# Feed-forward activations turned by transposing DMAs out of 16-bit halves instead of on TensorE

## The reference

```python
x = embeddings                                   # (8, 1024, 512) f32
x = layernorm(x + attention(x, w_qkv))
# feed-forward, I = 1408; fq = blockwise FP4 quantise and dequantise, 16 values per scale
gate = einsum('bsk,nk->bsn', fq(x), fq(w_gate))
up   = einsum('bsk,nk->bsn', fq(x), fq(w_up))
h    = silu(gate) * up
x = layernorm(x + einsum('bsk,nk->bsn', fq(h), fq(w_down)))
```

## Time and profile before

| what | value |
|---|---|
| median of 3 executions | 3875.96 us (3875.09 to 3875.98) |
| the profiled execution | 3875.39 us, its span 3873.6 us |
| PE busy | 3689.6 us, 95% of the span |
| DVE busy | 3168.6 us, 82% |
| POOL busy | 2203.6 us, 57% |
| ACT busy | 1711.3 us, 44% |
| granted TensorE clock, mean of the span | 0.989 of full speed |

### The profile page before, as it was taken

The page is one execution under the profiler, slowest core; times in us unless marked ns, Lnnn a source line. Parts: engine busy times, 40 slices in busy tenths (PEclk is TensorE's granted clock), DMA queues, the critical chain, the costliest instruction groups (busy, mean ns, idle before and its releaser), DMA issues.

```text
span 3873.6 us, 60731 instructions
## 1 busy us (share of the span) xinstructions
PE 3689.6 (95%) x22282; PEld 1713.6 (44%) x22469; DVE 3168.6 (82%) x5203; ACT 1711.3 (44%) x3084; POOL 2203.6 (57%) x1395
## 2 busy tenths in 40 slices
PE   3599999999999999999999999999999999999999
PEld 2244454344544445443554445434454345544354
DVE  9877888778877788778877788777887778877887
ACT  2166523664246632566226652366424663256622
POOL 1289623984249832698228962388424983269822
PEclk9699999999999999999999999999999999999999
DMA  5211101011011110111101110101101111010110
GB/s 171 79 39 31 58 20 39 18 41 50 23 34 30 38 47 20 41 27 31 52 25 37 32 58 20 39 18 42 50 23 34 30 38 47 20 41 26 34 49 23
DMA packets 106551, 152.38 MB, mean 39 GB/s; under 512 B 28176, under 2 KB 55568, under 8 KB 106128
## 3 DMA queue, kind: packets, MB, share of 16 engines
q1 hardware_dynamic: 106256, 148.49, 12.4%
HBM read 76.28 MB, written 19.66 MB: 25 GB/s over the span
## 4 chain that ended last, share of the span: by engine, by line
PE 76%; DVE 13%; issue 2%; ACT 2%; POOL 2%; DMA 1%; SPq 0%; DVEq 0%; ACTq 0%; POOLq 0%
PE SC L1646 15%; PE CT L1586 10%; PE R L699 9%; PE SC L1571 8%; PE R L679 7%; DVE mx L605 6%; PE CT L1668 6%; PE R L1668 6%; PE R L1646 5%; PE R L689 4%; PE R L711 2%; PE R L1606 2%; PE R L721 1%; POOL wd L1168 1%; DVE split L599 1%
## 5 line engine op out<-in xcount | busy, mean ns | idle before, releaser
L605 DVE TENSOR_REDUCE mx<-R 128x1 f32<-128x512 f32 x2080 | 1315.1, 683 | 344.6 <-PE R L699 339.9
L1285 ACT ACTIVATE arena<-SC 128x512 f32<-128x512 f32 x1364 | 756.6, 602 | 351.1 <-PE SC L1571 321.2
L1646 PE MATMUL SC<-wgu,split 128*128 128x512 f16 (+1 forms) x3456 | 714.5, 361 | 0.0
L1168 POOL TENSOR_TENSOR wd<-wd,arena 128x1024 f32<-128x1024 f32 x224 | 535.1, 2414 | 77.2 <-DVE wd L1407 77.2
L1194 POOL TENSOR_TENSOR arena<-arena,sc_h 128x704 f32<-128x704 bf16 (+1 forms) x144 | 178.4, 1253 | 605.7 <-DVE arena L528 605.7
L1646 PEld LDWEIGHTS SC<-wgu,split 128*128 128x128 f16 x3456 | 338.0, 98 | 331.6
L1327 ACT ACTIVATE arena<-SC,gain 128x512 f32<-128x512 f32 (+1 forms) x192 | 125.2, 652 | 810.1 <-PE R L1646 411.7
L1285 ACT ACTIVATE wd<-SC 128x512 f32<-128x512 f32 x684 | 387.5, 602 | 200.4 <-PE SC L1571 188.3
L679 PE MATMUL R<-xT,wqkv 128*128 128x512 bf16 x1509 | 398.2, 382 | 27.7 <-DVE xT L592 14.8
L699 PE MATMUL R<-ks_even,qs_even 96*128 96x512 bf16 x1056 | 394.9, 389 | 18.1 <-DVE mx L605 8.3
L699 PE MATMUL R<-arena 96*128 96x512 bf16 x1024 | 374.0, 382 | 14.6 <-DVE xT L592 6.5
(11 more groups left out here) (139 smaller groups left out, 5397.0 us busy)
## 6 DMA issues: line engine op xcount, KB each, us to landing
x<-n_L_attn_embeddings_dram SPq DMA_DIRECT2D x136, 256.0 KB, 2.7
wd<-wd_kept SPq DMA_DIRECT2D x32, 512.0 KB, 5.6
out_dram<-x SPq DMA_DIRECT2D x64, 256.0 KB, 2.0
ks_even<-split SPq DMA_DIRECT2D x204, 64.0 KB, 2.0
qs_even<-split SPq DMA_DIRECT2D x408, 32.0 KB, 1.9
arena<-split SPq DMA_DIRECT2D x192, 64.0 KB, 2.0
arena<-split SPq DMA_DIRECT2D x384, 32.0 KB, 1.9
wd<-wd_kept SPq DMA_DIRECT2D x16, 384.0 KB, 7.2
```

The lines of the kernel that those rows point to most:

```text
L605: nc.vector.reduce_max(mx[:, j:j + 1], ring_of(ring, job)[:, :], AX_X).then_inc(max_done, 1)
L1168: nc.gpsimd.tensor_tensor(acc[u % 2][i], acc[u % 2][i], probs_of(s)[:, hs, :], ALU.add).then_inc(pool_sum, 1)
L1285: nc.scalar.activation(probs_of(s)[:, hd, :], SC[e % SLOTS][:, :], ACT.Exp, scale=SCALE).then_inc(exp_done, 1)
L1646: last = nc.tensor.matmul(GU[kk % 2][which][:, 0:w], xhT[i % 2][:, part_x * KH + k, :], wgu[:, part_w * KH + k, which * I + first:which * ...
```

## The change

The turns leave PE. q_x and q_h are split into halves while they still lie untransposed in SBUF: ACT copies the high half (`x_high`, `h_high`), POOL subtracts to get the low half (`low_x`, `low_h`, which were DVE's), and SP issues one transposing DMA for the two halves of x together (128 x 1024 of 16 bits) and one for each piece of h. The pieces of h are now 768 and 640 columns, so the DMAs are 128 x 1536 and 128 x 1280; in tiles 0 and 7 they are 1024, 1024 and 768 wide. `xs` lies over xn, and `hs` over a spare stretch of the arena. The orders of all five engines change with it. ACT runs `x_high(i+1)` after silu(i, 2) and both `h_high(i-1)` between silu(i, 0) and silu(i, 1). POOL runs scale_x(i+1), inverse_deviation of the output norm of tile i-2, low_x(i+1), inverse_deviation for x, scale_h of both pieces, low_h of both. SP runs the h turns of tile i-1, the x turn of tile i+1, then the load and the store. At the head, `x_high(0)` stands ahead of the context copy on ACT, and the DMA for x(0) stands behind `stack_maxima` on SP. Of the last tile's projections, the second follows down's second chunk and the rest the third. DVE's add of y is earlier in the last tile.

```diff
-H_PIECES = (slice(0, I // 2), slice(I // 2, I))
+H_PIECES = (slice(0, 6 * P), slice(6 * P, I))
...
+        xs = xn.bitcast(F16)
+        hs = spare.bitcast(BF16)
...
+                    def turn_x(i):
+                        i += TILES * b
+                        sp.wait_ge(xs_lo, i + 1)
+                        if i >= 2:
+                            sp.wait_ge(gu_done, len(CHUNKS) * (i - 1))
+                        sp.dma_start_transpose(xhT[i % 2], xs).then_inc(xhT_loaded, 16)
+
+                    def turn_h(i):
+                        i += TILES * b
+                        for n, (first, k) in enumerate(tile_pieces(i)):
+                            sp.wait_ge(hs_lo, pieces(i)[n][0] + 1)
+                            if i >= 2 and n == 0:
+                                sp.wait_ge(y_done, i - 1)
+                            sp.dma_start_transpose(hT[i % 2][:, 2 * first:2 * (first + k), :],
+                                                   hs[:, 2 * first * P:2 * (first + k) * P]).then_inc(hT_loaded[n], 16)
+
+                    turn_x(0)
                     keep_x(0)
-                    for c in range(len(CHUNKS)):
+                    load_down(b, 0)
+                    turn_x(1)
+                    for c in range(1, len(CHUNKS)):
                         load_down(b, c)
-                    for i in range(TILES):
+                    keep_x(1)
+                    for i in range(1, TILES):
+                        turn_h(i - 1)
                         if i + 1 < TILES:
+                            turn_x(i + 1)
                             keep_x(i + 1)
...
+                def low_x(i):
+                    pool.wait_ge(xs_hi, i + 1)
+                    nc.gpsimd.tensor_tensor(xs[:, H:2 * H], q_x, xs[:, 0:H], ALU.subtract).then_inc(xs_lo, 1)
...
+                def low_h(i, n):
+                    k, cols = pieces(i)[n]
+                    high, low = halves_of(cols)
+                    pool.wait_ge(hs_hi, k + 1)
+                    nc.gpsimd.tensor_tensor(hs[:, low], q_h[:, cols], hs[:, high], ALU.subtract).then_inc(hs_lo, 1)
...
+                def x_high(i):
+                    act.wait_ge(qx_done, i + 1)
+                    nc.scalar.activation(xs[:, 0:H], q_x, ACT.Copy).then_inc(xs_hi, 1)
+
+                def h_high(i, n):
+                    k, cols = pieces(i)[n]
+                    act.wait_ge(qh_done, k + 1)
+                    if i >= 1 and n == 0:
+                        h_turned(act, i - 1)
+                    nc.scalar.activation(hs[:, halves_of(cols)[0]], q_h[:, cols], ACT.Copy).then_inc(hs_hi, 1)
...
                     if c == 0 and which == 0:
-                        pe.wait_ge(xhT_done, i + 1)
+                        pe.wait_ge(xhT_loaded, 16 * (i + 1))
...
+                        if k == at:
+                            pe.wait_ge(hT_loaded[n], turned_until(i, n))
```

More of the change, by code:

```diff
@@ L384, in in_chunks, with tile_pieces, turned_until, halves_of @@
             return i % TILES in (0, TILES - 1)
+        def tile_pieces(i):
+            return [(c.start // P, (c.stop - c.start) // P) for _, c in pieces(i)]
+        def turned_until(i, n):
+            b, i = divmod(i, TILES)
+            return 16 * ((TILES if n < len(H_PIECES) else 2) * b + 1 + (i if n < len(H_PIECES) else i // (TILES - 1)))
+        def halves_of(cols):
+            w = cols.stop - cols.start
+            return slice(2 * cols.start, 2 * cols.start + w), slice(2 * cols.start + w, 2 * cols.stop)
+        def h_turned(eng, i):
+            for n in range(len(pieces(i))):
+                eng.wait_ge(hT_loaded[n], turned_until(i, n))
         def rounds_before(i):
@@ L447, in post_ln_block @@
         qh_done = sem("qh_done")
-        hT_hi = sem("hT_hi")
-        hT_done = sem("hT_done")
+        hs_hi = sem("hs_hi")
+        hs_lo = sem("hs_lo")
+        hT_loaded = [sem(f"hT_loaded{n}") for n in range(len(CHUNKS))]
         y_done = sem("y_done")
@@ L1219, in tiles @@
                             inverse_deviation("out", at + i - 2)
+                        if 1 <= i < TILES - 1:
+                            low_x(at + i + 1)
                         if 1 <= i < TILES - 2:
                             inverse_deviation("x", at + i + 2)
-                        for n in range(len(pieces(at + i))):
-                            scale_h(at + i, n)
+                        if in_chunks(i):
+                            for n in range(len(CHUNKS)):
+                                scale_h(at + i, n)
+                                low_h(at + i, n)
+                        else:
+                            for n in range(len(H_PIECES)):
+                                scale_h(at + i, n)
+                            for n in range(len(H_PIECES)):
+                                low_h(at + i, n)
                     for i in range(TILES - 3, TILES):
@@ L1350, in tiles @@
-                        if i > at:
-                            h_out(i - 1, 2)
-                        if i + 2 < at + TILES:
-                            first_norm(i + 2)
-                    i = at + TILES - 1
-                    h_out(i, 0)
-                    second_norm(i - 2)
+                        if i + 2 <= last:
+                            first_norm(i + 2)
+                    silu(last, 0)
+                    for n in range(len(pieces(last - 1))):
+                        h_high(last - 1, n)
@@ L1453, in units @@
                             first_moments(TILES * b + 1)
[L1455 to L1462, removed]
-                    nc.vector.tensor_tensor(hT[i % 2][:, first + tiles:first + 2 * tiles, :],
-                                            ring_tiles(ring, ("hT", i, c), tiles),
-                                            hT[i % 2][:, first:first + tiles, :], ALU.subtract).then_inc(hT_done, 1)
                 def quantise_h(i, cols):
```

192 lines of the change are left out of this document (61 added, 131 removed).

## The result

The changed kernel takes 3805.12 us (3804.19 to 3807.41 in 4 runs) against 3875.55 us of the kernel before beside it (3875.09 to 3875.98, 4 runs). The ratio is 0.982 (0.9808 to 0.9832): 70.4 us or 1.8% faster, where I had forecast 30 us. The profiled execution took 3805.33 us, its span 3803.6 us.

A forecast was written before the change was run, and what follows sets the result against it. PE was taken as the bound, DVE a close second. Per batch 2.6 - 0.44 + 6 x (22.5 - 23.15) - 2.4 = -4.1 us, -33 over 8 batches; forecast 3846 us, range 3775 to 4070.

The forecast's parts named there:

- PE alone sets the pace: Rival, middle tiles: DVE and POOL pass more freely, period 21.4 us from PE's matmuls, 3790 us; chance 0.13.
- The period: Middle tiles, gate_up to gate_up: 22.5 us instead of 23.15, or 22.85 with the dearer POOL price.
- DVE's own sum: DVE per middle tile: 18.2 us bare work, 3.3 of waits and some 0.5 more of stalls, 22.0 us.
- DVE and POOL shut each other out: Middle tiles: small scalar instructions and SBUF passes wait for POOL, and POOL for them; 3.3 us of waits, formerly 0.75.
- POOL's price: POOL's added subtractions per tile: 1.65 and 1.4 us for the pieces of h, 1.2 for x.
- The landing time L: Transposing DMA of 256 KB inside SBUF, from issue to landing: taken as 3.0 us.
- the transposing DMA becomes the wait: Rival, gate_up(i+1) behind turn_x(i+1): slower if L exceeds about 4.3 us; 3968 at L = 6, 4044 at 7.2; chance 0.36.
- its extreme: Transposing DMA paid block by block: 30 blocks of a tile take 39 us, kernel about 1000 us slower.
- 18.9 + L: Middle-tile period in the DMA rival, with stalls, as the chain to turn_x plus landing time; break-even at L near 4.3 us.
- The head: Start of a batch's feed-forward part: gate_up(0) waits for the x(0) turn, 2.6 us later; tile 0 saves 0.44.
- The tail: After gate_up(7) of a batch: six turn groups go from PE, saving 2.4 us.
- the forecast of -4.1: Sum per batch of head, tile 0, six periods and tail: -4.1 us, -33 us over 8 batches.

The follow-up runs named there:

- experiment 2: Changed kernel with low_h subtracting only the first 128 columns of each piece in the middle tiles: 3802.48 us, ratio 0.9813.
- experiment 1: Changed kernel plus one unused POOL addition in each middle tile: behind low_h 3845.17 us (the slow kernel), behind scale_x 3805.96 us.
- experiment 3: Changed kernel with the unused POOL addition behind low_h, and low_x moved ahead of the output norm's inverse_deviation on POOL: 3834.81 us, ratio 0.9895.
- experiment 5: Changed kernel with every x turned on TensorE, DVE making its low half, and only h by transposing DMA: 3822.74 us, ratio 0.9866.
- experiment 4: Changed kernel with heads altered three ways: 14 unused matmuls in PE's gap, 3791.61 us; x(0) turn first on SP, 3780.85; x(0) turned on TensorE, 3772.96.

## Why the prediction was wrong

The direction was right, the mechanism of the stalls is there, and the size was off by 40 us. The rival *PE alone sets the pace* (0.13 in my chances, 3790 us) is what happened in the period, though not for its reason: DVE and POOL did shut each other out. Of the 15 us between its 3790 and the measured time 13 are the clock at the heads, which neither form had.

**The period: 22.5 forecast, 21.38 measured.** This is the step that failed. Laid out from gate_up(i) at 0 (992.40 in PE's timeline), my schedule and the trace:

| step | forecast | measured |
|---|---|---|
| scale_h twice begins | 5.1 | 5.16 |
| low_h twice ends | 11.3 | 10.84 |
| L522 (before, L516) ends | 11.4 | 10.88 |
| five passes end | 14.5 | 13.85 |
| second_moments ends | 16.6 | 16.05 |
| inverse_deviation ends | 18.0 | 17.39 |
| low_x ends | 19.3 | 18.50 |
| turn of x issued | 19.4 | 18.53 |
| landed | 22.4 | 21.25 |

The order and each releaser are as I had them. The terms are mis-sized, all to the same side: low_h ends 3.0 us behind scale_h where I had 3.4 (7.9 to 11.3), and with it the shut-outs are 2.4 us where I had 3.3; low_x 1.16 with no gap ahead of it where I had 1.3; landing 2.7 where I had 3.0. Together they are 1.1 us, which is the whole distance between the forecast period and PE's. DVE's own sum, 22.0 in the forecast, was 20.4, and the round of DVE and POOL 21.5. Below 21.4 a shorter round gives nothing (experiment 2), and a longer one costs in full (experiment 1), so the forecast stood on the steep side of a corner and the kernel at the corner itself, 0.1 us past it. The six periods gave -10.4 us a batch instead of -3.9.

**DVE and POOL shut each other out:** right as a mechanism. L518 and L522 of the scales of x are at means of 0.54 and 0.72 us, L520, with the instructions of that width for h counted in, at 0.99, and experiments 1 and 3 make the stalls larger on demand. They reach PE only in the last periods, where I had them in every one. Between quantise_h and low_x I expected some 0.5 us of stalls; at 1011.31 L518 took 0.23 us, so it was near nothing.

**POOL's price:** I took the middle of two rows, 1.65, 1.4 and 1.2 us. Measured: 3.00 for both pieces, 1.16 for x. The lower bound, by the scaling row, was the nearer.

**The landing time L:** 3.0 forecast, 2.7 measured for the 256 KB of x, and a median of 3.8 for the wider pieces of h, which have 4.4 us and more. The rival *the transposing DMA becomes the wait*, with 0.36 the largest beside the forecast, needed L near 4.3 and is refuted; so is its extreme. (By its own 18.9 + L the break-even is at 4.1; 4.3 goes with 18.6 + L, which is also what its 24.6 at L = 6 uses.) The Trainium skill's 1309 ns for one block, read block by block ("VectorE: DVE Perf Modes", section "The three transpose paths"), would make 8 blocks of x 10.5 us, an estimate by that page, and the trace has 2.7 for all 8. The Trainium skill's other reading, 261 GB/s ("DMA: Bandwidth & Descriptors", section "Latency and other measured facts"), is not at odds with x: by it 1.0 us of the 2.7 would be the transfer, an estimate. The pieces of h would need 0.3 to 0.5 us more by it, an estimate too, and took 1.1 more in the median, two of them issued one behind the other. The packets under 512 B did grow tenfold, from 28,000 to 281,000. The stores' 3.4 us, for which nobody on the path waits, is not the price of that number: in experiment 5, with the turns of h alone and still 213,008 such packets, stores land in 2.0 us again. It goes with the turn of x, which SP issues 1.9 us ahead of each store.

**The head:** I had gate_up(0) 2.6 us later; counted from where PE would now be free, 0.44 us earlier, that is a gap of 3.0 to 3.1, and 2.97 to 3.14 were measured. What I did not have is the clock, a term that the sum put at nothing: 1.5 us in this batch, 13.2 us in the eight heads, 13.5 by experiment 4. Of tile 0, +1.07 is just 1.5 - 0.44.

**The tail:** -2.4 us a batch forecast. The stretch from gate_up(7) to the next head holds this and the head's +2.6, together +0.2; measured were +0.68 in this batch and +0.3 in the mean, so the forecast holds. What moves single batches was not traced.

Summed against the forecast of -4.1, for this batch: -6.5 for the periods, +1.5 for the clock, +0.5 in the last stretch, -8.6.

## What to carry to other kernels

Where two or three resources are within a microsecond of each other, the period is the largest of several sums, and each must be bounded separately: errors that all fall on one side moved the bound from the chain to PE here. One of the sums can be a round that closes on two engines which both show idle time: DVE idled 1.0 to 1.7 us a tile, and with POOL it was full. After the chain is laid out, ask what happens if every term is a little cheaper, and not only dearer.

Work moved off TensorE to DMAs pays in the steady state, where the landing time lies under other work, and costs at the head of a stage, where nothing does. Turning the one head tile on TensorE and the rest by DMA gave 32 us more than turning all alike.

A wait of PE is to be priced with what the clock takes after it. Here a gap of 3 us cost about half as much again, or more, in 29 of 40 heads.

## What the runs showed of the hardware that I had not expected

- After an idle of 3.0 us TensorE's clock fell to 0.50 in 8 heads of 8 of one kernel, and in 3, 5, 6 and 7 of 8 of others with gaps as long; what decides it was not found. After 1.3 to 1.5 us it never did, and 14 unused matmuls in the gap (3.18 us) kept it at 1.00 and made the whole 13.5 us faster.
- The shut-out between DVE and POOL goes both ways, and more of it came with more work: in experiment 3 POOL's addition took 1.71 us instead of 1.27 while DVE's instructions beside it took up to 1.83.
- Issuing a transposing DMA holds SP's queue for 1.2 us (x) and 1.4 us (h) in the median, at most 2.3, against 0.4 to 0.6 for the load and the store (1.23 for L1126, 3.20 for the two of L1134, 0.58 for L1115 in the timeline of SP). In a period SP had the time.
- A store of 256 KB issued 1.9 us behind a transposing DMA landed in 3.4 us in the median; without that DMA, and with 144 other transposing DMAs in the kernel, in 2.0 us.
